# Count matmuls in two half-height pieces, the sample weight in the mask, Gram matmuls that alternate between halves, and a ScalarE step in the pooled sums

## The chip, the cores and the metric

The kernel runs on one core of a Trainium2 chip. The metric is the device time of one execution in microseconds (us); lower is better. TensorE (PE) multiplies, VectorE (DVE) and ScalarE (ACT) do elementwise work, GpSimd (POOL) issues indirect gathers, and SyncE (SP) issues most transfers.

## The reference, cut to what matters

A recommendation model for 2048 samples. Each of 26 tables (12500 rows of 64 numbers) is looked up at 20 indices per sample and the 20 rows are summed. A bottom network makes one more vector of 64. All pairs of the 27 vectors of a sample are multiplied, and a top network turns the products into one number.

```python
x = _mlp(dense_x, bot, sigmoid_last=False)                       # 13 -> 512 -> 256 -> 64
pooled = jax.vmap(lambda tab, ix: jnp.take(tab, ix, axis=0).sum(axis=1))(tables, indices)
Tcat = jnp.concatenate([x[:, None, :], jnp.transpose(pooled, (1, 0, 2))], axis=1)
Z = jnp.einsum('bim,bjm->bij', Tcat, Tcat)
R = jnp.concatenate([x, Z[:, li, lj]], axis=1)                   # li, lj: below the diagonal
return _mlp(R, top, sigmoid_last=True)                           # 415 -> 512 -> 256 -> 1
```

## The kernel before, in words

Twenty-one tables (TP) are pooled by matmul and five (TG) by gather. For the 21, the kernel counts how often each sample asks for each row, and multiplies the table by the counts.

**A table** lies in SBUF as 128 partitions x 98 rows, cut in seven chunks, split into a high and a low fp16 part (`parts`; `make_hi`, `subtract_hi`, `make_lo`). The 2048 samples are four blocks of 512. **A block's counts** come in 22 units of four groups of six samples (the last unit has two groups). For one group, 6 x 20 = 120 indices lie on 120 partitions. VectorE makes `onehot_p` (which of the 128 partitions the row lies in) and `onehot_c` (which of 33 columns, times a weight of the column's third, in the place of the sample). One matmul of `onehot_p` as weights and the 6 x 33 = 198 columns of `onehot_c` gives the group's counts (`count_unit`, L647). ScalarE turns a unit from PSUM into bytes (`unpack_unit`, L788). VectorE works in pairs of units (`onehot_pair`, L994 and L998), with two buffers; once per block it makes `weighted_c` in two steps (`weight_columns`, L980 and L982).

**A block's sum** is 98 matmuls of `parts` by the counts, 512 columns each (`sum_rows`, L664), into one of two accumulators. `phase(t, k, tn, kn)` interleaves the sum of one block with the counts of the next: 21 times four count matmuls and four sum matmuls, then two count matmuls and the last 14 sum matmuls. TensorE waits in front of a unit for its one-hots (`onehots_ready`), for the counts two units back to be unpacked (`counts_ready`), and at the start of a block for the accumulator (`acc_free`). VectorE scales the low half of a summed block (L1006), adds the scaled high half (L1009) and frees the accumulator (`pool_bags`).

**The gathers.** POOL issues 80 indirect gathers beside each table (`gather_piece`, L588), five to a piece; VectorE sums each piece (`sum_piece`, L1032), 16 pieces per table. POOL may be one bag of four pieces ahead (`piece_free`).

**The last part** has no table loop. In four tiles of 512 samples (r = 0 to 3) the kernel multiplies all slots of a sample (`make_grams`, L728): 64 partitions of `slots` hold one half of a tile's samples, 64 the other. A batch b is eight matmuls of one half; even batches are the lower half, odd ones the upper; a tile has 16 batches. Three pairs of PSUM banks rotate (`b % 3`). ScalarE copies two quarters of a batch out, VectorE the two others (`take_diagonals`, L376). SyncE moves the products through DRAM into `feats` (`move_pairs`), and `top_mlp(r - 1)` runs after `make_grams(r)`; the top network has the two remaining banks. In the profile each fp32 matmul is two records.

Each engine runs its program in the order written; nothing reorders it.

## Time and profile before

| | |
|---|---|
| median of 3 runs | 3101.85 us (3100.75 to 3103.76) |
| the profiled execution's own time | 3101.67 us |
| its span, first to last instruction | 3099.8 us |
| granted TensorE clock, mean over the span | 0.956 of full speed |
| table loop, one table | 126.56 us, 20 repeats |
| first Gram matmul after the loop | 2767.55 us |

"Busy" is the time in which an engine has an instruction in work. Matmuls are pipelined, so their records overlap; the distance from one start to the next says what one costs. "Idle before, releaser" is the gap ahead of an instruction and what ended it. A name such as `120x1584` is partitions x elements; `64*128` of a matmul is rows and columns of weights.

### The profile page before, as it was taken

The numbers are of one execution on the slowest core, as the hardware profiler recorded it, in microseconds if no ns is written. First come the engines' busy times: TensorE is split into PE (matmuls) and PEld (weight loads), VectorE is DVE, ScalarE is ACT, GpSimd is POOL, SyncE is SP. The second block draws the span as 40 slices with busy tenths as digits, with TensorE's granted clock in tenths as the row PEclk, the third lists the DMA queues.
The fourth block names the chain that finished last, engine by engine and source line by source line (L and its number), as shares of the span: only waits on it lengthen the run. The fifth ranks groups of instructions, "written<-read, shape, count | busy, mean of one in ns | idle before, by whom it ended". The sixth has DMA issues, their size and how long they took to land.

```text
span 3099.8 us, 50958 instructions
## 1 busy us (share of the span) xinstructions
PE 2968.0 (96%) x16980; PEld 1728.8 (56%) x16980; DVE 2566.2 (83%) x3442; ACT 1864.5 (60%) x2391; POOL 2051.5 (66%) x1639
## 2 busy tenths in 40 slices
PE   6999999999999999999999999999999999999999
PEld 2455555555555555555555555555555555569774
DVE  4599999999999999999999999999999999833221
ACT  3566757667576676666766757667576676622222
POOL 3278878787787887888888888888888888000000
PEclk8899999999999999999999999999999999985668
DMA  2112122122121221212212112122121221064411
GB/s 65 60 27 69 35 62 71 25 72 67 29 69 25 71 67 30 69 26 70 71 25 69 50 46 71 24 71 67 29 69 27 69 69 24 25 97 81 75 28 28
DMA packets 165642, 164.47 MB, mean 53 GB/s; under 512 B 108859, under 2 KB 127083, under 8 KB 160231
## 3 DMA queue, kind: packets, MB, share of 16 engines
q1 hardware_dynamic: 114135, 110.94, 13.0%
q0 software_dynamic: 51200, 52.53, 8.6%
q10 hardware_dynamic: 272, 0.52, 0.1%
q8 instruction: 23, 0.38, 0.1%
q14 instruction: 12, 0.10, 0.0%
HBM read 143.83 MB, written 20.05 MB: 53 GB/s over the span
## 4 chain that ended last, share of the span: by engine, by line
PE 57%; DVE 33%; issue 7%; ACT 2%; DVEq 1%; DMA 0%; SPq 0%; POOL 0%; ACTq 0%; POOLq 0%
PE ps L664 31%; PE ps L647 13%; DVE onehot_c L998 11%; PE ps L728 7%; PE ps L614 5%; DVE rowmax L928 4%; DVE onehot_p L994 4%; DVE weighted_c L982 3%; DVE weighted_c L980 3%; DVE pooled_sb L1006 2%; DVE pooled_sb L1009 1%; DVE rows L1032 1%; DVE bags_out L1032 1%; ACT counts L788 1%; ACT parts L767 0%
## 5 line engine op out<-in xcount | busy, mean ns | idle before, releaser
L588 POOL DMA_INDIRECT rows<-in_L_rec_tables,look x1600 | 2034.6, 1272 | 547.2 <-issue 484.0
L664 PE MATMUL ps<-counts,parts 128*128 128x512 fp8e3 x8232 | 2158.0, 388 | 0.0
L788 ACT CAST counts<-ps 128x792 int32<-128x792 f32 (+1 forms) x1848 | 1511.5, 824 | 886.2 <-PE ps L647 877.2
L664 PEld LDWEIGHTS ps<-counts,parts 128*128 128x128 f16 x8232 | 778.9, 96 | 596.6 <-issue 0.8
L647 PE MATMUL ps<-onehot_c,onehot_p 120*128 120x198 bf16 x7224 | 956.9, 252 | 90.4 <-DVE onehot_c L998 79.8
L647 PEld LDWEIGHTS ps<-onehot_c,onehot_p 120*128 120x128 bf16 x7224 | 659.6, 98 | 624.1 <-ACT counts L788 137.5
L998 DVE TENSOR_TENSOR onehot_c<-weighted_c,sample_mask 120x1584 bf16<-120x1584 bf16 x924 | 902.7, 977 | 0.0
L994 DVE TENSOR_TENSOR onehot_p<-iota_by_unit,place 120x1024 bf16<-120x1024 bf16 x924 | 634.9, 687 | 211.9 <-PE ps L647 186.2
L376 DVE COPY zt<-ps 32x208 f32<-32x208 f32 x128 | 87.5, 683 | 189.2 <-PE ps L728 188.3
L728 PE MATMUL ps<-slots 64*128 64x104 f32 x1024 | 220.3, 464 | 2.9 <-DMA slots<-pooled 2.9
L728 PEld LDWEIGHTS ps<-slots 64*128 64x128 f32 x1024 | 219.6, 365 | 4.9 <-DVE w_top1T L398 3.1
L1032 DVE TENSOR_REDUCE rows<-rows 128x64 f32<-128x384 f32 (+1 forms) x240 | 189.2, 788 | 0.0
L376 ACT COPY zt<-ps 32x208 f32<-32x208 f32 x128 | 63.4, 496 | 190.1 <-PE ps L728 189.4
L956 DVE SCALAR_TENSOR_TENSOR raw<-raw,coef_next,parts 128x896 f32<-128x896 f32 x147 | 168.7, 1148 | 3.2 <-ACT parts L760 1.8
L928 DVE TENSOR_REDUCE rowmax<-raw 128x1 f32<-128x896 f32 x147 | 155.8, 1074 | 0.0
L760 ACT ACTIVATE parts<-raw,coef_next 128x896 f16<-128x896 f32 x147 | 152.6, 1038 | 0.0
L980 DVE TENSOR_TENSOR weighted_c<-iota_by_unit,place 120x2904 bf16<-120x2904 bf16 x84 | 140.2, 1669 | 3.9
L982 DVE TENSOR_TENSOR weighted_c<-weighted_c,place 120x2904 bf16<-120x2904 bf16 x84 | 140.4, 1671 | 2.9
L767 ACT ACTIVATE parts<-raw 128x896 f16<-128x896 f32 x147 | 139.4, 948 | 0.0
L1006 DVE TENSOR_SCALAR pooled_sb<-ps,coef 64x512 f32<-64x512 f32 x84 | 63.5, 756 | 29.7 <-PE ps L664 27.0
L603 POOL MEMSET slots<- 128x1280 f32 x2 | 2.3, 1164 | 100.7 <-PE ps L664 100.7
L614 PE MATMUL ps<-feats,w_top0T 128*128 128x512 f32 (+1 forms) x128 | 67.4, 667 | 0.0
(82 smaller groups left out, 559.6 us busy)
## 6 DMA issues: line engine op xcount, KB each, us to landing
raw<-in_L_rec_tables SPq DMA_DIRECT2D x21, 1792.0 KB
raw<-in_L_rec_tables SPq DMA_DIRECT2D x21, 1344.0 KB
rows<-in_L_rec_tables,look POOLq DMA_INDIRECT x1600, 2.8
pooled<-pooled_sb SPq DMA_DIRECT2D x84, 128.0 KB, 2.3
slots<-pooled SPq DMA_DIRECT2D x30, 352.0 KB, 7.9
products<-zt SPq DMA_DIRECT2D x16, 351.0 KB
idx_raw<-in_r_indices SPq DMA_DIRECT2D x21, 159.4 KB
gathered<-bags_t SPq DMA_DIRECT2D x42, 64.0 KB
```

Source lines behind the costliest of these rows:

```text
L588: nc.gpsimd.indirect_dma_start(rows[:, s, l, :], None, rows_flat, bass.IndirectOffsetOnAxis(ap=look[:, c, s * PL + l:s * PL + l + 1].bitca ...
L614: last = nc.tensor.matmul(into[i % len(into)][0:mm, :], w, x, start=(k == 0), stop=(k == len(terms) - 1))
L647: last = nc.tensor.matmul(unit_ps[u % 2][:, x, 0:GC], onehot_p[:, r, sub, :, lane], onehot_c[:, r, sub, :, :, lane].rearrange("p c s -> p ...
L664: mm = nc.tensor.matmul(acc[k % 2][:, 0:NB], parts[:, j, :], count_bytes[k % 2][:, j % COLS, 0:NB, j // COLS], start=(j == 0), stop=(j == ...
L728: last = nc.tensor.matmul(banks[2 * (b % 3) + x // 4][:, x % 4 * P:x % 4 * P + GW], tile[:, g, :, :].rearrange("p k s -> p (k s)"), tile[: ...
L788: nc.scalar.copy(counts[k % 2][:, :, u * UG * GS:(u * UG + g) * GS].rearrange("p c (g s) -> p g c s", s=GS), unit_ps[u % 2][:, 0:g, 0:GC]. ...
L928: nc.vector.tensor_reduce(rowmax[:, q:q + 1], raw[:, q * CJ:(q + 1) * CJ, :], AX.XY, ALU.max, apply_absolute_value=True).then_inc(rowmax_p ...
L980: tt(weighted_c[:, :, :, :], iota, by_unit(1), ALU.is_equal).then_inc(weighted, 1)
L982: tt(weighted_c[:, :, :, :], weighted_c[:, :, :, :], by_unit(2), ALU.mult).then_inc(weighted, 1)
L994: tt(onehot_p[:, r, :, :, :], iota, at, ALU.is_equal)
L998: tt(onehot_c[:, r, :, :, :, :].rearrange("p u c s g -> p (u c) s g"), cols, mask, ALU.mult).then_inc(onehots_ready, 1)
L1032: nc.vector.tensor_reduce(dst, src, AX.X, ALU.add).then_inc(piece_free, 1)
```

## The change

The partitions are used in two halves of 64. Each half holds three samples of a group (60 indices), so a count matmul becomes two: rows 0 to 59 and rows 64 to 123, with 3 x 33 = 99 columns each, into two different banks. The weight of the column's third is multiplied into the sample mask (`weighted_s`, 3 samples wide) in place of the columns, so `weighted_c` becomes `column_c` and needs one large step. The index load becomes three transfers, and its conversion three steps. The low half of a pooled sum moves from VectorE to ScalarE (`take_lo`), and VectorE's half of it goes from pair 1 to pair 3 of a block. The Gram matmuls go sample by sample between the lower and the upper half, two batches at a time, with four pairs of banks, of which the last is the top network's: so each waits for the other.

```diff
-    GS = P // L
-    GC = GS * COLS
+    HALVES = 2
+    HS = P // HALVES // L
+    HK = HS * L
+    HP = P // HALVES
+    HC = HS * COLS
+    GS = HALVES * HS
@@ buffers
-        unit_ps = [ps[:, 2 * i:2 * i + 2, :].rearrange("p b (h c) -> p (b h) c", h=2) for i in range(2)]
+        unit_ps = [ps[:, 2 * i:2 * i + 2, 0:UG * HC] for i in range(2)]
@@ count_unit
-                    last = nc.tensor.matmul(unit_ps[u % 2][:, x, 0:GC], onehot_p[:, r, sub, :, lane],
-                                            onehot_c[:, r, sub, :, :, lane].rearrange("p c s -> p (c s)"),
-                                            start=True, stop=True)
-                last.then_inc(unit_counted, 1)
+                    for h in range(HALVES):
+                        rows_h = slice(h * HP, h * HP + HK)
+                        last = nc.tensor.matmul(unit_ps[u % 2][:, h, x * HC:(x + 1) * HC],
+                                                onehot_p[rows_h, r, sub, :, lane],
+                                                onehot_c[rows_h, r, sub, :, :, lane].rearrange("p c s -> p (c s)"),
+                                                start=True, stop=True)
+                        if g == units_of(u)[-1]:
+                            last.then_inc(unit_counted, 1)
@@ make_grams
-                for b in range(r * GRAMS_PER_TILE, (r + 1) * GRAMS_PER_TILE):
-                    half, w = b % 2, b % GRAMS_PER_TILE // 2
-                    if b >= 3:
+                for b in range(r * GRAMS_PER_TILE, (r + 1) * GRAMS_PER_TILE, 2):
+                    if b >= 4:
                         pe.wait_ge(diag_act, b - 2)
                         pe.wait_ge(diag_dve, b - 2)
+                    if r >= 2 and b == r * GRAMS_PER_TILE + 2:
+                        pe.wait_ge(top_act, TOP_STEPS * (r - 1))
                     for x in range(GRAMS):
-                        g = GRAMS * w + x
-
-                        last = nc.tensor.matmul(banks[2 * (b % 3) + x // 4][:, x % 4 * P:x % 4 * P + GW],
-                                                tile[:, g, :, :].rearrange("p k s -> p (k s)"),
-                                                tile[:, g, :, 1:SLOTS], start=True, stop=True)
-                    last.then_inc(grams_ready, 1)
+                        g = b % GRAMS_PER_TILE // 2 * GRAMS + x
+                        for half in range(2):
+
+                            last = nc.tensor.matmul(
+                                banks[2 * ((b + half) % 4) + x // 4][:, x % 4 * P:x % 4 * P + GW],
+                                tiles[half][:, g, :, :].rearrange("p k s -> p (k s)"),
+                                tiles[half][:, g, :, 1:SLOTS], start=True, stop=True)
+                            if x == GRAMS - 1:
+                                last.then_inc(grams_ready, 1)
@@ top_mlp
+                done = GRAMS_PER_TILE * min(r + 2, TILES)
+                pe.wait_ge(diag_act, done)
+                pe.wait_ge(diag_dve, done)
@@ ScalarE, called after unit 1 of the counts of block k + 2; for block 3 after the loop body's last unpack
+            def take_lo(t, k):
+
+                n = BLOCKS * t + k
+                act.wait_ge(block_summed, n + 1)
+                act.wait_ge(pooled_free, n + 1)
+                act.wait_ge(coef_adopted, t + 1)
+                nc.scalar.activation(pooled[:, :], acc[k % 2][D:2 * D, 0:NB], ACT.Copy,
+                                     scale=coef[D:2 * D, 1:2]).then_inc(lo_taken, 1)
@@ weight_columns
-                tt(weighted_c[:, :, :, :], iota, by_unit(1), ALU.is_equal).then_inc(weighted, 1)
-                dve.wait_ge(weighted, 2 * n + 1)
-                tt(weighted_c[:, :, :, :], weighted_c[:, :, :, :], by_unit(2), ALU.mult).then_inc(weighted, 1)
+                tt(column_c[:, :, :, :], iota, by_unit(1, COLS), ALU.is_equal).then_inc(weighted, 1)
+                tt(weighted_s[:, :, :, :], mask, by_unit(2, HS), ALU.mult).then_inc(weighted, 1)
@@ onehot_pair
-                whole = [GK, 2 * SUBS * COLS, GS, LG]
-                cols = weighted_c[:, 2 * SUBS * d:2 * SUBS * (d + 1), :, :].rearrange("p u (c a) g -> p (u c) a g", a=1).to_broadcast(whole)
+                whole = [P, 2 * SUBS, COLS, HS, LG]
+                cols = column_c[:, u, :, :].rearrange("p u (c a) g -> p u c a g", a=1).to_broadcast(whole)
+                mask = weighted_s[:, u, :, :].rearrange("p u (a s) g -> p u a s g", a=1).to_broadcast(whole)
@@ pool_bags
-                dve.wait_ge(block_summed, n + 1)
-                dve.wait_ge(pooled_free, n + 1)
-                nc.vector.tensor_scalar(pooled[:, :], acc[k % 2][D:2 * D, 0:NB], coef[D:2 * D, 1:2], None,
-                                        ALU.mult).then_inc(lo_taken, 1)
                 dve.wait_ge(lo_taken, n + 1)
```

**TensorE, the first units of a phase.** Before, ahead of the first sum of a block (waits are the ISA rows; L647 counts, L664 sums):

```order
L657 REGISTER_ALU
L660 ISA
L640 ISA
L642 ISA
L647 MATMUL ps<-onehot_c,onehot_p 128x198 x4
L664 MATMUL ps<-counts,parts 128x512 x4
```

Now (L659 counts, L678 sums):

```order
L671 REGISTER_ALU
L674 ISA
L650 ISA
L652 ISA
L659 MATMUL ps<-onehot_c,onehot_p 128x99 x8
L678 MATMUL ps<-counts,parts 128x512 x4
```

The order of the work and of the waits is the same; four matmuls of 198 columns became eight of 99 between two runs of four sums.

**VectorE, the end of the loop body**, where the last block of a table is taken from the accumulator. Before:

```order
L994 TENSOR_TENSOR onehot_p<-iota_by_unit,place 120x1024
L998 TENSOR_TENSOR onehot_c<-weighted_c,sample_mask 120x1584
L1006 TENSOR_SCALAR pooled_sb<-ps,coef 64x512
L1009 SCALAR_TENSOR_TENSOR pooled_sb<-ps,coef,pooled_sb 64x512
L963 COPY coef<-coef_next 128x2
```

Now:

```order
L1037 TENSOR_TENSOR onehot_p<-iota_by_unit,place 128x1024
L1042 TENSOR_TENSOR onehot_c<-column_c,weighted_s 128x792
L1048 SCALAR_TENSOR_TENSOR pooled_sb<-ps,coef,pooled_sb 64x512
L1005 COPY coef<-coef_next 128x2
```

The step L1006 has left VectorE; L1048 stands in its place and waits for ScalarE.

**ScalarE, the same place** (L782 is `make_hi`, L820 the unpack, L811 the moved step), now:

```order
L820 CAST counts<-ps 128x2x4x33x3
L780 REGISTER_ALU
L782 ACTIVATE parts<-raw,coef_next 128x14x64
L817 ISA
L820 CAST counts<-ps 128x2x4x33x3
L808 REGISTER_ALU
L811 ACTIVATE pooled_sb<-ps,coef 64x512
```

The moved step stands behind the unpack of units 0 and 1 of the next block and a `make_hi` between them, which stood there before too.

## Rows read from the trace of the kernel before

**Rows 1.** Busy time per engine in one table; stretch, PE, PEld, DVE, ACT, POOL, clock, DMA share, GB/s.
```profile
1441.70:1568.26 126.56, 122.19 (x744) 68.64 (x742) 117.99 (x157) 83.96 (x106) 102.23 (x81) 1.00 0.20 53
```

**Rows 2.** Timeline of TensorE, inside a block: start, us, instructions.
```profile
1201.88 1.07 PE L664 MATMUL ps<-counts,parts 128*128 128x512 fp8e3 x4
1202.79 0.52 PE L647 MATMUL ps<-onehot_c,onehot_p 120*128 120x198 bf16 x4
1203.15 1.07 PE L664 MATMUL ps<-counts,parts 128*128 128x512 fp8e3 x4
```

**Rows 3.** Groups by shape, same table; busy us, mean ns | idle before, releasers.
```profile
L588 POOL DMA_INDIRECT rows<-in_L_rec_tables,look x80 | 101.9, 1274 | 24.2 <-issue 23.9 <-DVE rows L1032 0.3
L788 ACT CAST counts<-ps 128x792 int32<-128x792 f32 x85 | 70.9, 840 | 42.3 <-PE ps L647 42.1
...
L998 DVE TENSOR_TENSOR onehot_c<-weighted_c,sample_mask 120x1584 bf16<-120x1584 bf16 x45 | 44.0, 977 | 0.0
...
L994 DVE TENSOR_TENSOR onehot_p<-iota_by_unit,place 120x1024 bf16<-120x1024 bf16 x44 | 30.2, 686 | 7.3 <-PE ps L647 6.0 <-DVE pooled_sb L1009 0.7
...
L982 DVE TENSOR_TENSOR weighted_c<-weighted_c,place 120x2904 bf16<-120x2904 bf16 x4 | 6.7, 1671 | 0.1
...
L1006 DVE TENSOR_SCALAR pooled_sb<-ps,coef 64x512 f32<-64x512 f32 x4 | 3.0, 756 | 0.1
```

**Rows 4.** Timeline of TensorE in the bottom network, beside the first count units.
```profile
51.35 0.53 PE L647 MATMUL ps<-onehot_c,onehot_p 120*128 120x198 bf16 x4
51.81 1.12 PE L614 MATMUL ps<-xT,w_bot0T 13*128 13x512 f32 x2
52.87 0.53 PE L647 MATMUL ps<-onehot_c,onehot_p 120*128 120x198 bf16 x4
```

**Rows 5.** Timeline of TensorE in the top network, single matmul records.
```profile
3072.95 0.59 PE L614 MATMUL ps<-feats,w_top0T 128*128 128x512 f32 x1
...
3073.38 0.59 PE L614 MATMUL ps<-feats,w_top0T 128*128 128x512 f32 x1
...
3073.90 0.69 PE L614 MATMUL ps<-feats,w_top0T 31*128 31x512 f32 x1
```

**Rows 6.** Chain that ended last, one Gram tile; Gram records in two short stretches.
```profile
2904.82 55.32 PE ps L728 x256
...
2988.68:2989.10 0.42, 0.42 (x3) 0.42 (x2) 1.00 0.00 0
...
2991.20:2991.62 0.42, 0.42 (x7) 0.42 (x5) 0.50 0.00 0
```

**Rows 7.** Groups by shape, 2800 to 3100 us: VectorE's copies of the products.
```profile
L376 DVE COPY zt<-ps 32x208 f32<-32x208 f32 x112 | 76.5, 683 | 170.3 <-PE ps L728 169.5
```

**Rows 8.** SyncE's timeline in the last part; one top network run by engine.
```profile
2822.94 14.31 SPq L489 DMA_DIRECT2D slots<-pooled  x8
...
2855.29 9.72 SPq L512 DMA_DIRECT2D feats<-products  x29
...
2877.05:2904.82 27.77, 26.21 (x53) 9.38 (x53) 1.02 (x2) 6.40 (x9) 0.00 (x0) 0.93 1.10 156
```

**Rows 9.** POOL's gathers: ns min/median/max; the longest kind, and VectorE beside it.
```profile
L588 POOL DMA_INDIRECT rows<-in_L_rec_tables,look x1600: 938/1172/3760, 46.4 to 2636.9; - x178
...
1521.53 3.75 POOL L588 DMA_INDIRECT rows<-in_L_rec_tables,look  x1 [0.30 <-issue]
...
1524.38 0.82 DVE L1032 TENSOR_REDUCE rows<-rows 128x64 f32<-128x384 f32 x1
```

**Rows 10.** A piece's last gather and VectorE's sum of it, early and 18 tables later.
```profile
264.08 0.94 POOL L588 DMA_INDIRECT rows<-in_L_rec_tables,look  x1 [0.30 <-issue]
...
284.11 0.71 DVE L1032 TENSOR_REDUCE rows<-rows 128x64 f32<-128x320 f32 x1
...
2550.94 1.41 POOL L588 DMA_INDIRECT rows<-in_L_rec_tables,look  x1 [0.30 <-issue]
...
2561.58 0.71 DVE L1032 TENSOR_REDUCE rows<-rows 128x64 f32<-128x320 f32 x1
```

More of the change, by code:

```diff
@@ L74, in build @@
     assert B % NB == 0 and UNITS % 2 == 0 and BLOCKS % 2 == 0 and SPAN % CHUNKS == 0
[L75 removed]
+    assert UG * HC <= BANK and L < 32 and GROUPS <= P and 2 * D == P and SLOTS <= QUAD
     assert TP * ROWS + ABSENT <= T * ROWS
@@ L214, in build @@
         parts = sb(loop, "parts", [P, SPAN, 2 * D], F16)
-        onehot_p = sb(loop, "onehot_p", [GK, 2, 2 * SUBS, P, LG], BF16)
-        onehot_c = sb(loop, "onehot_c", [GK, 2, 2 * SUBS, COLS, GS, LG], BF16)
-        weighted_c = sb(loop, "weighted_c", [GK, UNITS * SUBS, COLS, LG], BF16)
+        onehot_p = sb(loop, "onehot_p", [P, 2, 2 * SUBS, P, LG], BF16)
+        onehot_c = sb(loop, "onehot_c", [P, 2, 2 * SUBS, COLS, HS, LG], BF16)
+        column_c = sb(loop, "column_c", [P, UNITS * SUBS, COLS, LG], BF16)
+        weighted_s = sb(loop, "weighted_s", [P, UNITS * SUBS, HS, LG], BF16)
         NI = BLOCKS * GROUPS
-        idx_t = sb(loop, "idx_t", [GK, NI], F32)
-        scratch = sb(loop, "scratch", [GK, NI], F32)
+        idx_t = sb(loop, "idx_t", [P, NI], F32)
+        scratch = sb(loop, "scratch", [P, NI], F32)
         NIP = NI + UNITS * UG - GROUPS
-        place_next = sb(loop, "place_next", [GK, 3, NIP], BF16)
-        place = sb(loop, "place", [GK, 3, NIP], BF16)
+        place_next = sb(loop, "place_next", [P, 3, NIP], BF16)
+        place = sb(loop, "place", [P, 3, NIP], BF16)
         look = sb(loop, "look", [P, GB, L], I32)
@@ L552, in _ @@
             nc.gpsimd.memset(ident[:, :], 0.0).then_inc(const_step, 1)
-            nc.gpsimd.iota(iota_p[:, :], pattern=[[0, 1]], base=0, channel_multiplier=1,
-                           allow_small_or_imprecise_dtypes=True).then_inc(const_step, 1)
+            for h in range(HALVES):
+                pool.wait_ge(const_step, h + 1)
+                nc.gpsimd.iota(iota_p[h * HP:(h + 1) * HP, :], pattern=[[0, 1]], base=0, channel_multiplier=1,
+                               allow_small_or_imprecise_dtypes=True).then_inc(const_step, 1)
+            pool.wait_ge(const_step, HALVES + 1)
             nc.gpsimd.memset(idx_f, float(ABSENT)).then_inc(const_step, 1)
-            pool.wait_ge(const_step, 3)
+            pool.wait_ge(const_step, 4)
             nc.gpsimd.affine_select(out=ident[:, :], in_=ident[:, :], compare_op=ALU.not_equal, fill=1.0,
@@ L718, in make_grams @@
                 pe.wait_ge(slots_in[r % 2], 16 * loads)
[L719 to L721 removed]
+                tiles = [slots[r % 2][half * D:(half + 1) * D, :, :, :].rearrange("p k s g -> p g k s")
+                         for half in range(2)]
+                for b in range(r * GRAMS_PER_TILE, (r + 1) * GRAMS_PER_TILE, 2):
+                    if b >= 4:
                         pe.wait_ge(diag_act, b - 2)
                         pe.wait_ge(diag_dve, b - 2)
[L724 removed]
+                    if r >= 2 and b == r * GRAMS_PER_TILE + 2:
+                        pe.wait_ge(top_act, TOP_STEPS * (r - 1))
                     for x in range(GRAMS):
[L726 to L731 removed]
+                        g = b % GRAMS_PER_TILE // 2 * GRAMS + x
[6 more added lines that the diff above has]
+                                last.then_inc(grams_ready, 1)
             def top_mlp(r):
@@ L770, in convert_indices @@
             def convert_indices(t):
-                act.wait_ge(idx_loaded, 32 * t + 32)
+                act.wait_ge(idx_loaded, 48 * t + 48)
                 nc.scalar.copy(idx_f[:, :, 0:TAIL * L], idx_raw[:, :, 0:TAIL * L]).then_inc(idx_converted, 1)
-                nc.scalar.copy(idx_f[0:GROUPS - 1, :, TAIL * L:], idx_raw[0:GROUPS - 1, :, TAIL * L:]
-                               ).then_inc(idx_converted, 1)
+                for cols in (slice(TAIL * L, HK), slice(HP, HP + HK)):
+                    nc.scalar.copy(idx_f[0:GROUPS - 1, :, cols], idx_raw[0:GROUPS - 1, :, cols]
+                                   ).then_inc(idx_converted, 1)
             def copy_bags(n):
```

77 lines of the change are left out of this document (44 added, 33 removed).

## The prediction

> **What bounds the kernel now.** I read the busy shares per table first, then TensorE's timeline, then the groups, then POOL against VectorE. In one table of 126.56 us three engines are almost full: TensorE is busy for 122.2 us, VectorE for 118.0, and POOL for 102.2 [rows 1]. POOL's gathers have 23.9 us of gaps called "issue" around them [rows 3], so POOL is in truth taken for 126 us too.
>
> TensorE's own need comes from starts: four count matmuls take 0.36 us (1202.79 to 1203.15) and four sums 0.91 (1201.88 to 1202.79) [rows 2]. A block is 21 units of 1.27, two counts (0.18) and 14 sums (3.2), so 30.0 us; four blocks are 120 us, with 0.5 us of transposes about 120.5. The table takes 126.56, so about 6 us per table are stalls, and VectorE is why: its 118 us lie unevenly (a row maximum here, a `weighted_c` of 1.67 us twice per block there), and TensorE waits for `onehot_c` at such places.
>
> POOL has no slack either. A piece's last gather ended at 265.0 and VectorE summed it at 284.1, so POOL was 19 us ahead; 18 tables later the same two are at 2552.35 and 2561.6, 9 us ahead [rows 10]. The lead melts by 0.55 us per table: POOL needs 127.1 us per table. A gather takes 0.94 us at least, 1.27 in the mean, and 3.75 at most [rows 3, 9]. The longest one (1521.53 to 1525.28) ends 0.9 us after VectorE reaches a reduction, an operation with one input [rows 9], as if it had stood until then and needed its 0.9 from there. So I read the gathers as waiting for VectorE's operations with two inputs. Free of that it would need 80 x (0.94 + 0.30) = 99 us; 28 us per table are this wait.
>
> **The change, part by part.**
>
> *VectorE.* Two shapes of one operation give its cost per element: 2904 elements take 1671 ns and 1584 take 977 [rows 3], which is 0.526 ns per element on 144 ns. So `onehot_c` with 792 elements costs 0.56 us in place of 0.98, and the small weight step of 264 elements 0.28 in place of 1.67; L1006 (0.76) goes. Per table 44 x 0.42 + 4 x 1.39 + 4 x 0.76 = 27 us go, and VectorE falls to 91 us. If the longer pattern of `onehot_c` ran at half the rate, it would stay at 0.98 and VectorE at 109 us: still under TensorE's need. `onehot_p` keeps its 0.69. Direct worth: the 6 us of stalls per table go whatever the matmuls cost, unless something else becomes late.
>
> *Count matmuls.* C is the time of a unit's counts between two runs of sums, 0.36 now. Eight matmuls of 99 columns take its place. 198 columns cost 0.09, so 99 cost about 0.045 to 0.05 each. If the two halves run side by side, four pairs take 0.20; if one after the other, eight take 0.38.
> To this comes what a change of height costs. Beside matmuls of 13 rows the same four counts take 0.46 (51.35 to 51.81), not 0.36, and the two 13-row records take 1.06 (51.81 to 52.87) [rows 4] where 512 columns take 0.43 in a run of full height [rows 5]: 0.2 us too much for the pair and 0.1 for the counts, so 0.3 us for two changes. Part of this is the weight load of fp32. The step from 128 to 31 rows alone is 0.52 against 0.43: 0.09 us [rows 5]. I take 0.09 per change; a unit has two: 0.18. So C is 0.38 with overlap, 0.56 without, 0.20 with overlap and free changes.
> The Trainium skill, TensorEngine Tiling (Array Packing), Key Properties, says that changing the tiling mode drains TensorE; the 0.09 us agree with this, and it speaks against the change. The same skill, TensorE: Matmul & The Clock Gate, Part 3, says that matmuls of different row groups run concurrently; no row here shows that, since the two halves never alternate before. By both pages the sum would be the 0.38 that the rows above bound.
>
> *A table then* is 88.8 (sums) + 86 C (21 1/2 units' counts in four blocks) + 0.5, plus 1.0 for the next point: 90.3 + 86 C. At 0.38 it is 123.0; break-even with 126.56 is C = 0.42; at 0.56 it is 138.5.
>
> *The moved step.* Where block 3 of a table is taken, L1048 on VectorE waits for ScalarE, which stands behind the unpacks of units 0 and 1 and a `make_hi`. From the phase's start: unit 0 counted 0.4, unpack 0.84 for 792 elements [rows 3], the `make_hi` of 896 elements about 0.95 at that rate, unpack 0.84, moved step about 0.76 (L1006's price; the unpack of 792 elements bounds it by 0.84, nothing in these rows from below), L1048 0.75, copy 0.2, the next pair 1.25: 6.0 us. TensorE wants that pair at unit 4, 5.1 us. Queued behind L1048 are that pair and all else of VectorE. So 1 us per table, 0 to 2. In the other blocks the step comes four units before VectorE needs it and costs nothing; ScalarE is busy for 84 of 126 us [rows 1] and has 3 us to spare.
>
> *Gram matmuls.* A tile's 256 records take 55.3 us, 0.216 each [rows 6]. They come in two speeds, three in 0.42 us and seven in 0.42 us, and the slow one is seen at full granted clock and the fast one at 0.50 [rows 6]; so the clock doesn't set it, and 0.14 us per record is reached with nothing overlapped between halves. With alternation I take 0.11 to 0.14, a tile of 28 to 36 us. VectorE needs 2 x 0.683 per batch [rows 7], 22 us per tile, and stays hidden. What follows is SyncE: at 28 us per tile it first issues the loads of the tile after next (2822.9 to 2844.1) and then moves products, whose last load is issued at 2865.0 [rows 8], 42 us after the Gram tile ended. Before, the next tile hid 54 of these. At 28 us the first top network waits some 16 us, and the four tiles give 4 x 27 - 16 = 93 us; at 36 us there is no wait left, and they give 4 x 19 = 77 us. The new wait of the top network for both batches' copies costs about 2.8 us, three times: 8. I take 80 us less in all. At unchanged 0.216 it is +8; were all records as slow as three in 0.42 (70 us a tile), +60.
>
> *Start and end:* one more index transfer and conversion ahead of the first counts, some 1 us; neglected.
>
> **Sum**, against the profiled execution, 3101.7 (the median of the runs is 3101.85): 20 tables x (123.0 - 126.6) = -71, Gram -80: **2951 us**.
>
> **Rivals.**
> 1. *The halves don't overlap, the change is slower.* The eight matmuls go one after the other and each unit pays two changes of height: C = 0.56, a table of 138.5 us, +240 in the loop, with the Gram gain 3260 us. For it: every record of a short matmul here pays a change of height, and none shows two at once. It decides from C = 0.47 on (the Gram gain of 80 us is then used up). Between 0.42 and 0.47 the loop loses and the whole still wins.
> 2. *Changes are cheap, and POOL becomes the bound.* With C under 0.29 TensorE would need 115 us or less, and POOL's gathers set the pace. Their 99 us stand; the 28 us of waiting shrink, as VectorE's one-hots and weights fall from 44 x 1.66 + 8 x 1.67 = 86 to 44 x 1.25 + 4 x 1.95 = 63 us per table: by the share 20 us remain, by the square of a pair's length 16. So a table is 115 to 119 us, -150 to -230 in the loop, and 2790 to 2870 in all.
>    The Trainium skill, SBUF — State Buffer, Who interferes with whom, says that a two-input operation of VectorE contends with a GpSimd instruction that reads SBUF; this case's gather of 3.75 us agrees, and by the rule the pace of POOL follows what VectorE does.
> 3. *Alternating Gram matmuls gain nothing* (the slow speed is that of strided reads, which alternate as well): 3030 us if the loop goes as forecast.
> 4. *The stalls return elsewhere*, at ScalarE's unpack (22 x 0.84, nine chunk steps of about 0.95 and the moved step are 28 us in a block of 30): up to 2 us per table, 2990 us.
>
> **How the numbers follow.** C of 0.30 to 0.42, overlap with paid changes, 40%: 2870 (POOL's floor) to 3020 with the Gram gain, and 2951 at C = 0.38. C under 0.30 and POOL the bound, 24%: 2770 to 2870. C of 0.42 to 0.50, 14%: 3020 to 3155, faster in half of it. C over 0.50, 22%: over 3150. The Gram gain fails in about 15% of each, which adds 80 us. The range of eight in ten is 2780 to 3200: it leaves out the worst half of the serial case and loops under POOL's estimated floor. The likeliest case's own range is 2870 to 3020. Faster by over 0.2% (about what a measurement of this kernel can tell from no change): 0.66; slower by over 0.2%: 0.30; within: 0.04.
>
> **What would show it.** Start to start, the eight count matmuls should take 0.38 us between two runs of four sums at 0.91; near 0.56 is rival 1, near 0.2 rival 2. A table's period says the rest: 123 us, and if it is longer than 90.3 + 86 C, somebody else is late; POOL's lead over VectorE's sums tells whether it is POOL. VectorE should be busy for 91 us per table, `onehot_c` take 0.56, and a gather under 1.2 in the mean. A Gram tile should take 28 to 36 us, with TensorE idle ahead of the first top network until its products land. Most likely to be wrong: the price of a change of height, which the rows show beside fp32 only, times 3600.

## The result and the profile after

The change makes the kernel 1.5% faster: 3054.01 us in the median of 4 runs (3052.93 to 3058.61) against 3101.3 us of the kernel before, ratio 0.985 [0.9833, 0.9867]. The prediction had 2951.

The profiled execution took 3058.61 us. Its page, in the parts that answer to the table of before (span 3099.8): the span, the busy shares, the chain that ended last by engine.

```profile
span 3056.8 us, 65500 instructions
...
PE 2934.3 (96%) x24204; PEld 1249.3 (41%) x24204; DVE 1991.5 (65%) x3358; ACT 2182.6 (71%) x2496; POOL 1759.3 (58%) x1640
...
PE 85%; ACT 7%; issue 5%; SPq 1%; DMA 1%; DVE 0%; ACTq 0%; POOL 0%; DVEq 0%; POOLq 0%
```

The same row of the page of before:

```profile
PE 57%; DVE 33%; issue 7%; ACT 2%; DVEq 1%; DMA 0%; SPq 0%; POOL 0%; ACTq 0%; POOLq 0%
```

VectorE, with 33% of the chain before, is hardly in it any more. Beside TensorE it is now ScalarE, for 7% of the span.

Busy time by engine, in one table of the loop (1380.60 to 1507.80) and in 1000 us of it, which answers to [rows 1]. Columns: stretch, its us, PE, PEld, DVE, ACT, POOL busy, granted clock, DMA share, GB/s.

```profile
1380.60:1507.80 127.20, 124.56 (x1077) 49.58 (x1076) 90.75 (x151) 98.11 (x110) 86.66 (x81) 0.99 0.21 54
...
1000.00:2000.00 1000.00, 978.71 (x8538) 390.14 (x8536) 721.29 (x1199) 776.19 (x862) 689.21 (x638) 1.00 0.21 55
```

VectorE fell from 118.0 to 90.8 us, as the prediction worked it out. But a table became longer, 127.2 for 126.56 us. TensorE now needs more: its busy time of 124.6 us is up from 122.2. And ScalarE went from 84 to 98.1.

TensorE's timeline inside a block, which answers to [rows 2]: start, us, instructions.

```profile
1200.05 0.37 PE L659 MATMUL ps<-onehot_c,onehot_p 60*128 60x99 bf16 x8
1200.35 1.07 PE L678 MATMUL ps<-counts,parts 128*128 128x512 fp8e3 x4
1201.36 0.36 PE L659 MATMUL ps<-onehot_c,onehot_p 60*128 60x99 bf16 x8
1201.65 1.07 PE L678 MATMUL ps<-counts,parts 128*128 128x512 fp8e3 x4
1202.66 0.37 PE L659 MATMUL ps<-onehot_c,onehot_p 60*128 60x99 bf16 x8
```

Start to start, the eight counts take 0.30 us (0.36 for four before), but the four sums take 1.01 (0.91 before): a unit is 1.304 for 1.27 (medians over the trace: 0.297 and 1.007). 84 such units take 109.5 us, the four ends of a block 13.9 (0.20 for the last counts and 3.26 for 14 sums, which were 3.16), the transposes 0.5. So TensorE's own need is 123.9 us per table (before 120.5), and 3.3 us are stalls (before 6).

The groups of the same 1000 us by shape, which answer to [rows 3]: busy us, mean ns | idle before, releasers.

```profile
L598 POOL DMA_INDIRECT rows<-in_L_rec_tables,look x630 | 687.7, 1092 | 307.6 <-issue 187.6 <-DVE rows L1071 120.0
L820 ACT CAST counts<-ps 128x792 int32<-128x792 f32 x661 | 647.4, 997 | 217.6 <-PE ps L659 214.2 <-issue 0.3
L1042 DVE TENSOR_TENSOR onehot_c<-column_c,weighted_s 128x792 bf16<-128x792 bf16 x346 | 195.3, 564 | 0.0
L1048 DVE SCALAR_TENSOR_TENSOR pooled_sb<-ps,coef,pooled_sb 64x512 f32<-64x512 f32 x32 | 23.6, 738 | 47.6 <-ACT pooled_sb L811 47.6
```

A gather takes 1.09 us instead of 1.27, and POOL now waits for VectorE's sums (`rows L1071`), 15 us per table: it is ahead and bounds nothing. ScalarE's unpack of the same 792 elements takes 1.00 us where it took 0.84. VectorE waits for ScalarE's low half (L811) 47.6 us in eight waits, once per table.

The place of that wait, in the timeline of all engines:

```profile
1389.67 1.03 ACT L782 ACTIVATE parts<-raw,coef_next 128x896 f16<-128x896 f32 x1
1390.61 0.97 ACT L820 CAST counts<-ps 128x792 int32<-128x792 f32 x1
1391.61 0.68 ACT L811 ACTIVATE pooled_sb<-ps,coef 64x512 f32<-64x512 f32 x1
...
1392.32 0.74 DVE L1048 SCALAR_TENSOR_TENSOR pooled_sb<-ps,coef,pooled_sb 64x512 f32<-64x512 f32 x1 [5.84 <-ACT pooled_sb L811]
...
1395.32 0.37 PE L659 MATMUL ps<-onehot_c,onehot_p 60*128 60x99 bf16 x8 [1.67 <-ACT counts L820]
```

VectorE stands for 5.84 us; behind it are `coef` and the next pair of one-hots, and TensorE stands for 1.67 us in front of the unit that needs them. The label names the unpack, which shares the wait; the one-hots, made from 1394.02 to 1395.19, are what came last.

In five of the 20 tables TensorE loses time a second time just behind this wait. Two stretches of the table above, with the granted clock as the third number from the end:

```profile
1392.00:1396.60 4.60, 2.93 (x26) 1.04 (x24) 3.50 (x6) 4.04 (x5) 0.94 (x1) 1.00 0.20 46
1396.70:1400.00 3.30, 3.30 (x23) 1.51 (x24) 3.30 (x6) 1.86 (x4) 0.16 (x1) 0.50 0.13 12
```

TensorE had stood for 0.75 us (at 1388.37) and 1.67 us (at 1395.32); from 1396.7 to 1400.1 its granted clock is the lower of its two levels (1.2 and not 2.4 GHz), and sums start 0.43 us apart in the place of 0.226. The five tables with such a stretch take 128.2 to 128.5 us, the others mostly 126.6 to 127.0. That is some 7 us in all, or 0.4 of the 3.3 us of stalls per table.

In the last part a Gram tile is shorter, which answers to [rows 6]; the chain of waits there:

```profile
2784.42 56.40 PE ps L745 x416
2842.99 2.50 SPq L514
2845.53 7.73 DMA products<-zt
...
2862.76 6.25 DMA feats<-products
2869.09 18.06 PE ps L624 x32
...
2897.70 34.80 PE ps L745 x256
```

256 records take 34.8 us where they took 55.3, 0.136 us each for 0.216. They start two at a time, one of each half, and such a pair every 0.27 us, which was the slow one of the two speeds of a single record before. The mean granted clock is about the same, 0.56 in this tile (2897.70 to 2932.50) and 0.53 in the one of before (2904.82 to 2960.14), and the pairs start 0.27 us apart in its first 4 us, at a granted clock of 1.00, as in the rest at 0.50. From the first Gram matmul (2784.4; before 2767.6) to the end of the span it is now 272.4 us, before 332.3. So the last part won 60 us, and the loop and what lies before it lost 17.

### The profile page after: what moved, and what is told of

It is laid out like the page before. It is cut to its first block, busy times and chain, and to the rows that moved or that the text cites. A ratio compares the mean times of both kernels' runs of the same rounds, so it can differ in the third digit from the quotient of the medians.

```text
span 3056.8 us, 65500 instructions
## 1 busy us (share of the span) xinstructions
PE 2934.3 (96%) x24204; PEld 1249.3 (41%) x24204; DVE 1991.5 (65%) x3358; ACT 2182.6 (71%) x2496; POOL 1759.3 (58%) x1640
## 4 chain that ended last, share of the span: by engine, by line
PE 85%; ACT 7%; issue 5%; SPq 1%; DMA 1%; DVE 0%; ACTq 0%; POOL 0%; DVEq 0%; POOLq 0%
PE ps L678 59%; PE ps L659 16%; PE ps L624 5%; PE ps L745 4%; ACT counts L820 4%; ACT parts L782 2%; ACT parts L789 1%; SPq L496 0%; ACT h_bot L833 0%; ACT pooled_sb L811 0%; SPq L519 0%; DMA look_in<-in_r_indices 0%; DMA pooled<-pooled_sb 0%; DMA products<-zt 0%; SPq L503 0%
## 5 line engine op out<-in xcount | busy, mean ns | idle before, releaser
L598 POOL DMA_INDIRECT rows<-in_L_rec_tables,look x1600 | 1745.2, 1091 | 834.3 <-issue 474.2
L820 ACT CAST counts<-ps 128x792 int32<-128x792 f32 (+1 forms) x1848 | 1773.0, 979 | 583.3 <-PE ps L659 571.1
L678 PE MATMUL ps<-counts,parts 128*128 128x512 fp8e3 x8232 | 2178.4, 390 | 0.0
L1037 DVE TENSOR_TENSOR onehot_p<-iota_by_unit,place 128x1024 bf16<-128x1024 bf16 x924 | 636.6, 689 | 639.1 <-PE ps L659 613.4
L678 PEld LDWEIGHTS ps<-counts,parts 128*128 128x128 f16 x8232 | 646.8, 96 | 755.6 <-issue 6.2
L659 PEld LDWEIGHTS ps<-onehot_c,onehot_p 60*128 60x128 bf16 x14448 | 382.4, 95 | 876.1 <-issue 758.2
L659 PE MATMUL ps<-onehot_c,onehot_p 60*128 60x99 bf16 x14448 | 666.5, 209 | 55.0 <-ACT counts L820 35.2
L1042 DVE TENSOR_TENSOR onehot_c<-column_c,weighted_s 128x792 bf16<-128x792 bf16 x924 | 521.7, 565 | 0.0
L1071 DVE TENSOR_REDUCE rows<-rows 128x64 f32<-128x384 f32 (+1 forms) x240 | 188.1, 784 | 9.0 <-DVE pooled_sb L1048 9.0
L1048 DVE SCALAR_TENSOR_TENSOR pooled_sb<-ps,coef,pooled_sb 64x512 f32<-64x512 f32 x84 | 62.0, 738 | 145.8 <-ACT pooled_sb L811 145.8
L782 ACT ACTIVATE parts<-raw,coef_next 128x896 f16<-128x896 f32 x147 | 155.8, 1060 | 1.0
L1024 DVE TENSOR_TENSOR column_c<-iota_by_unit,place 128x2904 bf16<-128x2904 bf16 x84 | 140.5, 1672 | 3.9
L745 PE MATMUL ps<-slots 64*128 64x104 f32 x1024 | 138.9, 456 | 4.2 <-DMA slots<-pooled 4.2
L745 PEld LDWEIGHTS ps<-slots 64*128 64x128 f32 x1024 | 138.2, 367 | 6.1 <-issue 6.1
L624 PE MATMUL ps<-feats,w_top0T 128*128 128x512 f32 (+1 forms) x128 | 68.5, 677 | 20.1 <-DMA feats<-products 15.4
L811 ACT ACTIVATE pooled_sb<-ps,coef 64x512 f32<-64x512 f32 x84 | 57.4, 683 | 26.1 <-PE ps L678 24.1
L613 POOL MEMSET slots<- 128x1280 f32 x2 | 2.3, 1165 | 120.8 <-PE ps L678 120.8
```

The lines of the kernel that those rows point to most:

```text
L598: nc.gpsimd.indirect_dma_start(rows[:, s, l, :], None, rows_flat, bass.IndirectOffsetOnAxis(ap=look[:, c, s * PL + l:s * PL + l + 1].bitca ...
L624: last = nc.tensor.matmul(into[i % len(into)][0:mm, :], w, x, start=(k == 0), stop=(k == len(terms) - 1))
L659: last = nc.tensor.matmul(unit_ps[u % 2][:, h, x * HC:(x + 1) * HC], onehot_p[rows_h, r, sub, :, lane], onehot_c[rows_h, r, sub, :, :, lan ...
L678: mm = nc.tensor.matmul(acc[k % 2][:, 0:NB], parts[:, j, :], count_bytes[k % 2][:, j % COLS, 0:NB, j // COLS], start=(j == 0), stop=(j == ...
L745: last = nc.tensor.matmul(banks[2 * ((b + half) % 4) + x // 4][:, x % 4 * P:x % 4 * P + GW], tiles[half][:, g, :, :].rearrange("p k s -> p ...
L782: nc.scalar.activation(parts[:, c, 0:D], raw[:, c, :], ACT.Copy, scale=coef_next[:, 2:3]).then_inc(hi_ready, 1)
```

## The experiments

What each gave, beside the kernel before on the same chip:

| kernel | median us | ratio to before | one table, us |
|---|---|---|---|
| the change | 3054.01 | 0.985 [0.9833, 0.9867] | 127.2 |
| gram_only | 3039.89 | 0.9796 [0.9773, 0.9819] | 126.5 |
| lo_back | 3022.39 | 0.974 [0.9718, 0.9763] | 125.3 |
| unpack_gchs | 3035.48 | 0.9781 [0.9758, 0.9804] | 126.2 |
| unpack_flat | 3034.09 | 0.9778 [0.9753, 0.9802] | 126.1 |
| lo_back_gchs | 3013.05 | 0.9707 [0.9684, 0.973] | 125.2 |
| halves_apart | 3070.63 | 0.9891 [0.9863, 0.9919] | 127.5 |
| full_height | 3025.48 | 0.9746 [0.9718, 0.9773] | 125.5 |
| lower_twice | 3361.69 | 1.0833 [1.0801, 1.0866] | 141.7 |
| full_mask | 3028.09 | 0.9758 [0.9736, 0.978] | 126.4 |
| full_mask_lo | 3038.9 | 0.9785 [0.9762, 0.9809] | 126.4 |
| bursts | 2923.18 | 0.9418 [0.9396, 0.944] | 120.8 |
| bursts_pairs_first | 2910.48 | 0.9377 [0.9356, 0.9399] | 120.8 |

The last column is the mean distance from one copy of `coef` on VectorE to the next, over the last 18 tables of the profiled execution (before: 126.5). The medians are of four runs, those of halves_apart, full_height and lower_twice of two.

The theory after the result: the Gram part gives 60 us; the loop gives nothing because each unit pays two changes of height, and because ScalarE, with a longer unpack and the moved step, took over the stalls that VectorE had caused. The rival: the stalls are not ScalarE's, but POOL's or those of the halves themselves, so that giving ScalarE's work back changes little. Letters such as A and B1 in the expectations are those of each expectation alone.

**gram_only.** The kernel before with the alternating Gram matmuls alone.

```diff
-                    half, w = b % 2, b % GRAMS_PER_TILE // 2
+                        g = b % GRAMS_PER_TILE // 2 * GRAMS + x
+                        for half in range(2):
...
-                        last = nc.tensor.matmul(banks[2 * (b % 3) + x // 4][:, x % 4 * P:x % 4 * P + GW],
...
+                            last = nc.tensor.matmul(
+                                banks[2 * ((b + half) % 4) + x // 4][:, x % 4 * P:x % 4 * P + GW],
```

> The kernel before with the alternating Gram matmuls alone; counts, mask and pooled sums as before. Theory: the last part is worth 60 us by itself, as the two traces have it (first Gram matmul to the end: 332 us before, 272 now), and the table loop (126.56 us per table) is untouched: 3041 us. Rival: the loop's shorter or longer end moves the last part's transfers, and part of the 60 us belongs to the loop: then 3055 to 3070.

3039.89 us, 61 less than the kernel before, with its 126.5 us per table unchanged. The Gram part is worth 61 us by itself, and all else that the change does costs 14 (3054.0 - 3039.9).

**lo_back.** The change, with the low half of the pooled sums back on VectorE, at pair 3.

```diff
-                nc.scalar.activation(pooled[:, :], acc[k % 2][D:2 * D, 0:NB], ACT.Copy,
-                                     scale=coef[D:2 * D, 1:2]).then_inc(lo_taken, 1)
...
+                dve.wait_ge(block_summed, n + 1)
+                dve.wait_ge(pooled_free, n + 1)
+                nc.vector.tensor_scalar(pooled[:, :], acc[k % 2][D:2 * D, 0:NB], coef[D:2 * D, 1:2], None,
+                                        ALU.mult).then_inc(lo_taken, 1)
```

> The changed kernel with the low half of the pooled sums back on VectorE, at pair 3 as now. Theory A (the moved step is what TensorE waits for at the handoff after block 3, together with the chunk steps): the table falls from 127.2 to about 125 us and the time by 40 us, to 3015. Theory B (the unpack, 0.98 us for a unit where it was 0.84, is what makes ScalarE late, and the moved step of 0.68 us four times per table is a small part of that): 126.5 us per table, 3040 us. If ScalarE had nothing to do with it: 3054.

31.6 us faster than the change, between the 40 of theory A and the 14 of theory B. The moved step was a loss, not a gain: 0.76 us of VectorE, which had 36 us to spare, became an item in the queue of the engine that was late.

**unpack_gchs and unpack_flat.** The unpack wrote, for each group and column, runs of three samples of one half, with the half as its outermost loop. unpack_gchs goes through both halves inside a group and column, so that six samples are written in a row, as before. unpack_flat writes straight on (another layout, other sums).

```diff
-                        "p c (g h s) -> p h g c s", h=HALVES, s=HS),
-                    unit_ps[u % 2][:, :, 0:g * HC].rearrange("p h (g c s) -> p h g c s", c=COLS, s=HS),
+                        "p c (g h s) -> p g c h s", h=HALVES, s=HS),
+                    unit_ps[u % 2][:, :, 0:g * HC].rearrange("p h (g c s) -> p g c h s", c=COLS, s=HS),
```

> The changed kernel with the unpack's elements taken in the order group, column, half, sample, so that the destination is written in runs of six and the source jumps between the halves. Same elements. Theory B1 (the destination's runs of three make the unpack slow): the unpack returns to 0.84 us, ScalarE is no longer late, the table falls to about 124.5 us, 3000 us. Theory B2 (runs of three in either operand cost it, so the source's jumps do as well): the unpack stays at 0.98 or grows, 3054 us or more.

> The changed kernel with the unpack writing the same number of elements one behind the other; the counts then lie in another order and the sums are of other samples, so it computes something else. It shows what the access pattern costs: if the unpack falls to 0.84 us or less, the pattern of the destination is the price, and the time shows what the loop would be with ScalarE early: 123.7 us of TensorE's own per table, 2985 us. If the unpack stays at 0.98, the source (two banks, or 128 partitions written by two matmuls) is the price, and the time stays at 3054.

The unpack's group in 1000 to 2000 us, first of unpack_gchs, then of unpack_flat:

```profile
L820 ACT CAST counts<-ps 128x792 int32<-128x792 f32 x667 | 555.4, 839 | 302.5 <-PE ps L659 301.7
```

```profile
L820 ACT CAST counts<-ps 128x792 int32<-128x792 f32 x669 | 543.8, 818 | 313.6 <-PE ps L659 312.7
```

The order alone brings the unpack from 1.00 back to 0.84 us and the kernel down by 18.5 us; the straight one, at 0.82, by 20. The elements, their types and their banks are the same, so the cost lay in the runs of three. Both expectations had the unpack right and the time too low (3000 and 2985 us): with the short unpack alone VectorE still waits 5.5 us per table for the moved step.

**lo_back_gchs.** Both at once.

> The changed kernel with both reliefs of ScalarE: the low half back on VectorE, and the unpack in the order group, column, half, sample. Theory: ScalarE is all that makes the table longer than TensorE's own 124.2 us, and the two gains (31.6 and 18.5 us) overlap in part because no more than 3 us per table can be had: 2995 to 3008. If they add in full: 3004. Rival (the rest of the stalls is of another kind): 3020.

3013.05: 41 us under the change, where the two apart gave 31.6 and 18.5. So they relieve the same place. A table is now 125.2, 2 us less than in the change, and that is what the stalls that ScalarE made were. It is still 1.3 us above TensorE's own 123.9, so the kernel is 5 us above the expected range: most of the rest stands once per table in front of the first unit of a block, a wait that the profile calls "issue" and that is not traced further.

**halves_apart, full_height, lower_twice.** What the count matmuls cost. halves_apart issues the four of the lower half first, then the four of the upper. full_height lets each of the eight run over all 124 rows (other sums). lower_twice lets all eight read the lower half (upper half not counted).

```diff
-                for g in units_of(u):
-                    x = g % UG
-                    sub, lane = u % 2 * SUBS + x // LG, x % LG
-                    for h in range(HALVES):
+                for h in range(HALVES):
+                    for g in units_of(u):
+                        x = g % UG
+                        sub, lane = u % 2 * SUBS + x // LG, x % LG
```

```diff
-                        rows_h = slice(h * HP, h * HP + HK)
+                        rows_h = slice(0, HP + HK)      # full_height
+                        rows_h = slice(0, HK)           # lower_twice
```

> The changed kernel with a unit's four lower count matmuls first and its four upper ones behind them. Theory (the two halves overlap only where they alternate): the eight take about 0.42 to 0.50 us from their first start to the sums' first where they take 0.29 now, a unit 1.45 to 1.50 us, the table 138 to 143 us, 3270 to 3400 us. Rival (a matmul of 99 columns costs 0.03 us by itself, halves or not): no change, 3054 us.

> The changed kernel with every count matmul over all 124 rows, so that no change of height and no overlap is left; both halves then count all six samples and the sums are other ones. Theory: eight matmuls of 99 columns one after the other, 0.05 us each, 0.39 us for a unit's counts and sums back at 0.905: unit 1.30 us, as now; so the overlap's gain is just what the two changes of height cost, and the time stays within 1% of 3054. Rival: short matmuls in full height are bound by their weight loads, above 0.06 us each, unit over 1.39, 3200 us.

> The changed kernel with all eight count matmuls of a unit over rows 0 to 59, so that the upper samples are never counted and the sums are other ones; heights change as now. Theory (two independent streams, one in each half of the rows, 0.054 us per matmul in each; the four lower and the four upper overlap in whatever order they are issued): one stream of eight takes 0.43 us to which the change out adds 0.08, 0.51 in all where it was 0.29 to 0.31; unit 1.52 us, table about 145 us, 3400 us. Rival (a matmul of 60 rows and 99 columns simply costs 0.027 us, halves or not): 0.30 us, 3054 us.

TensorE's count matmuls alone, from the start of a unit's first: the change, halves_apart, full_height, lower_twice. The second column is the stretch, the x the matmuls that had started by its end.

```profile
1200.05:1200.22 0.17, 0.17 (x8) 1.00 0.52 121
```

```profile
1199.79:1199.96 0.17, 0.17 (x7) 1.00 0.00 0
```

```profile
1199.86:1200.03 0.17, 0.17 (x4) 1.00 0.00 0
```

```profile
1200.22:1200.39 0.17, 0.16 (x4) 1.00 0.00 0
```

In 0.17 us eight start when they alternate, seven when they are issued four and four, and four when all are of full height or all in one half. So each half takes a matmul about every 0.05 us, and the two halves run beside each other, even where the program gives all of the lower half first. In halves_apart the lower half's last matmul, known by the semaphore that it raises, is the fourth in the program and the seventh to start (1199.952), so the words "nothing reorders it" ahead of the prediction don't hold for these starts. By a rule of strict order the upper half's first could not start before the lower half's fourth, 0.17 us in; the Trainium skill, TensorE: Matmul & The Clock Gate, Part 3 (The mechanism), states that rule ("MATMULs are pc-monotone in start AND end"), and for the starts the trace doesn't agree with it. My expectation of halves_apart rested on such an order and missed by 200 us and more. It is 17 us slower than the change, which is hardly clear of the noise between two chips (0.9863 to 0.9919 against 0.9833 to 0.9867). Of the 12 us between the profiled executions half arise before the third table and half in the 18 tables after it; its eight counts take 0.307 for 0.297. The rest is not explained.

full_height takes 0.38 for the eight (0.0475 each) and 0.91 for the sums, a unit of 1.29, and is 29 us (0.9%) faster than the change; I had expected 1.30 and a time within 1%. In lower_twice the eight take 0.48 and the sums again 1.01; I expected 0.51 and 3400 us. Eight matmuls of one half at 0.047 are 0.38, so a change of height costs 0.10 in the counts and 0.10 in the sums. By that price four pairs take 0.30 - 0.10, some 0.19 us, in the place of full_height's 0.38. The overlap of the halves saves 0.19 us per unit, and the two changes cost a little more, 0.2.

**full_mask and full_mask_lo.** The weight in the mask and the Gram part without the halves: count matmuls of full height and 198 columns as before. full_mask has the low half on VectorE at pair 1, full_mask_lo on ScalarE, at pair 3.

```diff
+                    last = nc.tensor.matmul(unit_ps[u % 2][:, x, 0:GC], onehot_p[:, r, sub, :, lane],
+                                            onehot_c[:, r, sub, :, :, lane].rearrange("p c s -> p (c s)"),
+                                            start=True, stop=True)
```

> The kernel before (full-height counts of 198 columns) with the alternating Gram matmuls and the weight in the mask, the low half on VectorE. Theory: TensorE's own 120.4 us per table stay, VectorE falls from 118 to 112.5 us, and the stalls of 6 us shrink to 3: 123.5 us per table, and 2980 us in all, faster than the changed kernel. Rival (stalls come from the row maxima beside the one-hots, not from the mean): 125.5 us, 3020 us.

> As the one before, with the low half on ScalarE and VectorE's half at pair 3, as in the changed kernel. Theory: VectorE at 109.5 us; ScalarE's unpack is 0.84 us here and has room: 122.5 us per table, 2960 us. Rival (the handoff at the table's last block costs what it saves): equal to the one before.

Both missed. full_mask is 12 us under gram_only, where 60 were expected for the freed VectorE. Waits of full_mask in 1000 to 2000 us (engine, tile and line waited for, us in total, times, longest), and its gathers:

```profile
DVE rows L1042 <- DMA rows<-in_L_rec_tables,look: 37.2, 8, 5.2
PE ps L648 <- DVE onehot_c L1009: 34.8, 23, 3.3
```

```profile
L589 POOL DMA_INDIRECT rows<-in_L_rec_tables,look x633 | 806.7, 1274 | 191.7 <-issue 191.7
```

Here POOL never waits for anybody, VectorE waits for the gathers' data once per table for 4.7 us, and TensorE waits for VectorE by about as much. 80 x (1.274 + 0.303) = 126.2 us and 0.4 for the one other step of the engine are POOL's pace. The tables show when it takes hold: the first three between copies of `coef` take 123.1, 123.0 and 123.0 us, as I had expected, and there is no wait for the gathers' data in the first of them; the 16 after them take 126.8 in the mean. So as soon as POOL's lead is used up, a gather of 1.27 holds the loop at what it was before, whatever the two other engines need. In the change a gather takes 1.09, and this limit is gone.

full_mask_lo is 11 us slower still, so the moved step is a loss here too. It never has the fast tables: its first two take 127.4 us and those from the third on 126.3, with VectorE waiting 3.0 us once per table for the low half from ScalarE. At the fifth copy of `coef` it is 16 us behind full_mask, and it wins half of this back once POOL holds full_mask at 126.8.

**bursts.** If two changes of height cost 0.175 us, as I took it by then, they should be paid less often. On lo_back_gchs, in the phases of blocks 1 and 2, the 16 count matmuls of two units go ahead of eight sums.

```diff
+                    if k in (1, 2):
+                        if u % 2:
+                            continue
+                        j1 = SPAN if u == UNITS - 2 else PER_UNIT * (u + 2)
+                        await_rows(t, k, PER_UNIT * u, j1)
+                        count_unit(tn, kn, u)
+                        count_unit(tn, kn, u + 1)
+                        for j in range(PER_UNIT * u, PER_UNIT * (u + 2)):
+                            sum_rows(t, k, j)
+                        continue
```

> As the one before, and in phases 1 and 2 of a table, where ScalarE has no chunk steps beside its unpacks, the counts of two units go in one run of 16 matmuls ahead of eight sums: half the changes of height there. Theory (a change in and out costs 0.095 + 0.08 us): 22 pairs of changes fewer per table, 3.9 us, 78 us in 20 tables: 2930 us. Rival (both PSUM buffers of the counts are then full at once, and TensorE waits for two unpacks of 0.84 us within 1.8 us of sums): the gain is eaten, 3010 or slower.

TensorE's timeline of it:

```profile
1236.30 1.98 PE L678 MATMUL ps<-counts,parts 128*128 128x512 fp8e3 x8
1238.21 0.56 PE L659 MATMUL ps<-onehot_c,onehot_p 60*128 60x99 bf16 x16
1238.70 1.98 PE L678 MATMUL ps<-counts,parts 128*128 128x512 fp8e3 x8
1240.61 0.56 PE L659 MATMUL ps<-onehot_c,onehot_p 60*128 60x99 bf16 x16
```

Two units take 0.49 + 1.91 = 2.40 us instead of 2.61, and each of the two blocks has eleven such pairs (the last one of a unit and a half): 22 x 0.21 = 4.6 us per table, 92 in all. Measured: 90 us, and a table of 120.8 for 125.2. This is the most direct proof of the price of a change, since no matmul is added or taken away, and it says how the price divides. Eight more counts in a row cost 0.19 us (0.297 to 0.490), 0.048 per pair, which leaves 0.10 of a unit's 0.30 for the change; four more sums cost 0.90 (1.007 to 1.909), which leaves 0.105. So two changes cost 0.21 us and not the 0.175 that the expectation took from the starts inside a unit: part of the price lies in the second pair of a unit, which starts 0.058 us behind the first, where later ones follow in 0.048. Beside it a gather takes 1.12 us, and POOL still waits for VectorE's sums: it does not bound at 120.8 either.

**bursts_pairs_first.** On bursts, SyncE moves the products of the first Gram tile before it loads the slots of the third.

```diff
+                if r == 0:
+                    move_pairs(0)
...
-                move_pairs(r)
+                if r:
+                    move_pairs(r)
```

> As the one before, with the products of the first Gram tile moved by SyncE before it loads the slots of the third. Theory: the first top network stands some 15 us for its products after the second Gram tile, since 21 us of load issues come first; this wait goes: 15 us less than the one before. Rival: the third tile's slots then land late, and the wait moves to the third Gram tile: no change.

12.7 us less, of 15 expected. The chain of its last part: both Gram tiles run through, and the top network, at 2722.84, waits for nothing but VectorE's copies.

```profile
2651.25 69.32 PE ps L758 x512
2720.57 0.48 DVE zt L381
...
2722.84 17.41 PE ps L627 x32
```

This is the best version: 6.2% faster than the kernel before, 4.7% faster than the change.

## Why the prediction was wrong, step by step

The sign was right, with more than three times the gain. Against the profiled executions the forecast was -151 us (-71 in the loop, -80 in the Gram part); it came to -43.

- **"`onehot_c` costs 0.56 us", "VectorE falls to 91 us"**: 0.564 and 90.8 measured. The small weight step costs 0.287. Right.
- **"So C is 0.38 with overlap"**: the halves do overlap, and the four pairs take 0.19 where 0.20 was taken. But the two changes cost 0.21 per unit where 0.18 was taken, so C, the unit less 0.905 for its sums, is 0.40, and the last runs of a block pay 0.1 each too. TensorE's need is 123.9 us, not the 122.0 that 88.8 + 86 x 0.38 + 0.5 gives: 1.9 us per table, **38 us in all**. The mechanism was right and the price of a change too small, the very term that the prediction called most likely to be wrong; a hundredth of a microsecond in C is 17 us of time. Rival 1, at 0.56, is out: lower_twice shows what it would have cost.
- **"The 6 us of stalls per table go whatever the matmuls cost"**, with 1.0 us left: this is the step that failed. 3.3 us are left, 2.3 more, **46 us in all**. VectorE was relieved, and its stalls went, but the engine behind it was not costed as changed: "ScalarE ... has 3 us to spare" took the unpack at 0.84 us. It is 1.00, and 22 of them take 3.5 us more per block, all of that spare. The step that moved there then made VectorE wait 6 us once per table, and TensorE 1.7 us after it; in five tables TensorE's lower granted clock behind that wait took some 1.5 us more, which no term had. That is rival 4 ("the stalls return at ScalarE's unpack, up to 2 us per table, 2990 us"), which had the place and the size right, and was given no chance of its own; and it came on top of the need. lo_back, unpack_gchs and lo_back_gchs show it: 41 us come back, 2 us per table, and no table of lo_back_gchs has the lower clock.
- **"So 1 us per table, 0 to 2"** for the moved step: lo_back gives 1.6 us per table (31.6 / 20) beside the long unpack, and 1.1 beside the short one (3035.48 - 3013.05 = 22.4 us). Within the bounds.
- **"Free of that it would need 99 us; ... 16 to 20 us remain"** for POOL: the gather fell to 1.092, which is (1.092 - 0.94) x 80 = 12 us of waiting. A table needs 111 us of POOL, and rival 2 did not arise. That POOL was already at the limit before, by a lead that melts, was read rightly: full_mask shows it. Why its gathers stay at 1.27, although one of the two large weight steps of a block is gone there as well, is open: either the waiting follows `onehot_c` (0.98 there, 0.56 in the change) much more than the weight steps, or another thing sets it.
- **Gram, "a tile of 28 to 36 us"**: 34.8 measured, and rival 3 is out. **"At 36 us there is no wait left"** failed: TensorE waits 15.4 us for the products. The 42 us run to where SyncE issues the last load. By that same count 42 - 34.8 leaves 7 us, and the 6.3 us in which the load lands were left out. 4 x 20.5 less 15.4 is 67, and the Gram part gave 61, which leaves some 6 us for the new waits for the copies (8 were taken). So 61 and not 80: **19 us**.

Together 38 + 46 + 19 = 103 of the 108 us between the forecast and the profiled execution. The other 5 lie ahead of the loop or in its ends, and are not traced further.

That a unit of 1.304 us is the sum of what it does and two changes of height is shown (full_height, lower_twice, bursts). That the runs of three cost ScalarE 0.16 us is shown by unpack_gchs. That the gathers shorten because VectorE's two-input operations do fits every run but full_mask and full_mask_lo, and is not shown.

## What to carry to other kernels

When an operation is made cheaper on one engine by laying its data out differently, look for the engine that reads or writes the new layout: the one-hots gained, and the unpack behind them paid. Count alternations and not only matmuls: where short matmuls of half height stand between full ones, make the runs longer before making the matmuls shorter. And a step is worth moving only off the engine that is late after the change, which is not the one that was late before.

## What the runs showed of the hardware

- At full granted clock, matmuls of 60 rows and 99 columns in two halves of the partitions start in pairs every 0.048 us (bursts, after, halves_apart), in whichever order the two halves are issued; in one half alone one starts every 0.047 us (lower_twice), and over 124 rows one every 0.0475 (full_height). The first step behind a change takes up to 0.058.
- A change between such matmuls and those of 128 rows costs 0.10 us in each direction, 0.21 for two (bursts). That a change of tiling mode drains TensorE is stated by the Trainium skill, TensorEngine Tiling (Array Packing), Key Properties; these numbers agree with it.
- Gram matmuls of 64 rows in fp32 that alternate between the halves take 0.136 us per record (34.8 us for 256) in the place of 0.216, at a mean granted clock of 0.56 and before of 0.53: the shorter time is not owed to a faster clock.
- ScalarE, writing 792 elements from PSUM: 0.82 us straight on, 0.84 in runs of six, 1.00 in runs of three.
- VectorE's price of 144 ns and 0.526 ns per element, read from two shapes of one operation before, held for a pattern of another shape: 0.561 against 0.564 us.
